# A two-block network on one core: the recurrence taken two tokens at a time, and a tail that keeps channels on partitions

## The reference

```python
w = jnp.exp(-jnp.exp(time_decay + jnp.tanh(xw @ td_w1) @ td_w2)).reshape(b, l, h, s_)
r, k, v = (xr @ Wr.T), (xk @ Wk.T), (xv @ Wv.T)          # each reshaped to (b, l, h, s_)
g = jax.nn.silu(xg @ Wg.T)
def step(s, rkvw):
    r_t, k_t, v_t, w_t = rkvw
    a = k_t[..., :, None] * v_t[..., None, :]
    out = jnp.einsum('bhi,bhij->bhj', r_t, u * a + s)
    s = a + w_t[..., :, None] * s
    return (s, out)
m = og.mean(-1, keepdims=True)                            # og: out, per head of 16 channels
va = ((og - m) ** 2).mean(-1, keepdims=True)
og = ((og - m) / jnp.sqrt(va + 1e-05)).reshape(b, l, e) * gn_w + gn_b
x1 = x + og * g @ Wo.T
xc = _ln(x1, ln2_w, ln2_b)
# shift by one token, two mixes xk2 and xr2, then:
rr = jax.nn.sigmoid(xr2 @ Wfr.T)
kk = jnp.square(jax.nn.relu(xk2 @ Wfk.T))
return x1 + rr * (kk @ Wfv.T)
```

## Time and profile before

| | us |
|---|---|
| median of 3 runs | 1902.09 (1901.77 to 1902.61) |
| the profiled execution, whole | 1903.22 |
| its span, first to last instruction | 1901.3 |

### The profile page before, as it was taken

How to read it: one execution, slowest core, us unless ns; L and a number is a source line. 1 busy time by engine, 2 the same in 40 slices (tenths; PEclk the granted TensorE clock), 3 DMA queues, 4 the chain that set the end, 5 groups by cost and what they waited for, 6 DMA issues and landing times.

```text
span 1901.3 us, 34866 instructions
## 1 busy us (share of the span) xinstructions
PE 1761.4 (93%) x12356; PEld 1228.6 (65%) x12356; DVE 1775.5 (93%) x2084; ACT 1196.1 (63%) x2849; POOL 1253.3 (66%) x822
## 2 busy tenths in 40 slices
PE   5888999999999999999999999999999999999866
PEld 3666676767666677766667776666776666676533
DVE  3599999999999999999999999999999999999981
ACT  3546666666666666666666666666666666666422
POOL 1246777676777767677777766777776677776541
PEclk8899999999999999999999999999999999999878
DMA  6233433333343333333333443333443333333320
GB/s 239 60 98 96 106 102 92 101 104 102 100 106 99 92 101 104 104 101 102 99 91 102 106 106 98 103 98 91 105 107 103 98 103 96 95 107 96 91 66 11
DMA packets 86203, 189.32 MB, mean 100 GB/s; under 512 B 18800, under 2 KB 35312, under 8 KB 85008
## 3 DMA queue, kind: packets, MB, share of 16 engines
q1 hardware_dynamic: 64528, 170.32, 33.7%
q10 hardware_dynamic: 21504, 16.78, 2.7%
HBM read 161.91 MB, written 16.78 MB: 94 GB/s over the span
## 4 chain that ended last, share of the span: by engine, by line
DVE 52%; issue 24%; POOL 11%; PE 7%; ACT 6%; DVEq 0%; DMA 0%; POOLq 0%; ACTq 0%; SPq 0%
DVE S L615 18%; DVE S L606 8%; DVE S L624 8%; POOL rstd L402 7%; ACT wrep L863 3%; DVE xf L578 3%; PE bank L1004 3%; DVE nmax L521 3%; DVE xx L568 2%; PE bank L1011 1%; DVE xin L531 1%; POOL rstd L400 1%; DVE st L663 1%; DVE x L659 1%; POOL S L446 1%
## 5 line engine op out<-in xcount | busy, mean ns | idle before, releaser
L615 DVE TENSOR_TENSOR_SCAN S<-wrep,S 128x1024 f32<-128x1024 f32 x256 | 602.6, 2354 | 2.1 <-ACT wrep L863 0.8
L446 POOL COPY S<-s 128x8 f32<-128x8 f32 x256 | 281.4, 1100 | 291.9 <-PE bank L1129 283.3
L624 DVE TENSOR_TENSOR S<-S,rT 128x1024 f32<-128x1024 f32 x256 | 343.3, 1341 | 2.8 <-ACT rT L868 1.6
L606 DVE TENSOR_TENSOR S<-vrep,kT 128x1016 f32<-128x1016 f32 x256 | 341.0, 1332 | 0.0
L430 POOL TENSOR_TENSOR xf<-xf,xa 128x512 f32<-128x512 f32 x160 | 249.3, 1558 | 89.8 <-DVE xf L578 87.5
L402 POOL TENSOR_TENSOR rstd<-rstd,mhalf 128x1 f32<-128x1 f32 (+1 forms) x96 | 211.3, 2201 | 8.0
L1129 PE MATMUL bank<-S,slide 128*32 128x256 f32 x2048 | 165.0, 394 | 23.8 <-DVE S L624 23.7
L827 ACT ACTIVATE bank<-bank,par 128x128 f32<-128x128 f32 x640 | 175.8, 366 | 10.6 <-PE bank L1085 10.6
L402 POOL TENSOR_TENSOR hrs<-hrs,mhalf 128x32 f32<-128x32 f32 x32 | 174.8, 5462 | 2.7
L400 POOL TENSOR_SCALAR rstd<-mv 128x1 f32<-128x1 f32 (+1 forms) x96 | 36.2, 377 | 204.9 <-DVE mv L542 151.8
L790 ACT ACTIVATE prob<-bank,nmax 128x512 f32<-128x512 f32 x128 | 88.3, 690 | 102.4 <-DVE nmax L521 101.5
(11 more groups left out here) (131 smaller groups left out, 3763.3 us busy)
## 6 DMA issues: line engine op xcount, KB each, us to landing
vrep<-v_dram SPq DMA_DIRECT2D x256, 512.0 KB
xc<-x_c SPq DMA_DIRECT2D x32, 256.0 KB, 6.4
xs<-x_s SPq DMA_DIRECT2D x32, 256.0 KB, 7.1
v_dram<-vT ACTq DMA_DIRECT2D x32, 256.0 KB, 2.3
xres<-xin SPq DMA_DIRECT2D x32, 256.0 KB, 6.1
out<-rr ACTq DMA_DIRECT2D x32, 256.0 KB, 2.0
Wv<-big_w SPq DMA_DIRECT2D x1, 1024.0 KB, 7.3
Wk<-big_w SPq DMA_DIRECT2D x1, 1024.0 KB, 9.3
```

The costliest lines, as they stand in the source:

```text
L446: po.tensor_copy(S[:, u % 2, :, 0], s0[:, p, k:k + UJ]).then_inc(pool_wkv.sem, 1)
L606: ve_.tensor_tensor(S[:, u % 2, :, 1:P], vrep[:, u % 2, :, 0:P - 1], k, ALU.mult).then_inc(dve_wkv.sem, 1)
L615: ve_.tensor_tensor_scan(s, wrep[:, u % C, :, :].rearrange("p j t -> p (j t)"), s, 0.0, ALU.mult, ALU.add).then_inc(dve_wkv.sem, 1)
L624: ve_.tensor_tensor(s, s, rT[:, p, u % C, :].unsqueeze(1).broadcast_to([P, UJ, P]), ALU.mult).then_inc(dve_wkv.sem, 1)
```

## The change

Three things are changed, and the orders written out by hand are redone to suit.

1. The recurrence runs over pairs of tokens. The outer products go into a tile `A` of 128 tokens, with the key of each first token already multiplied by the second token's decay (`mid_kw`); `wkv_pair` adds the two of each pair into a tile `S` of 64 columns; the scan runs over 64 pairs with the product of two decays (`ez2`, made on GpSimd, and a plain copy in `decay`); `wkv_read` reads each state twice, once with the receptance of the first token and once with that of the second times the first's decay (`mid_rw`), and writes into `A`. What the pair's first token gives the second directly (`rk2`) goes through `tail_C` with the bonus.
2. The tail keeps channels on partitions. The channels of a head are laid out in another order (`by_j`, by a permutation of `Wv`, `Wg`, `Wo` and the norm's parameters on the host), so that the bank of sums already has the wanted layout. The bonus is added to it on VectorE (`tail_o`, `tail_o2`, `tail_ob`, `tail_os`), the squares are summed over heads on TensorE (`tail_Vr`), ScalarE adds eps and spreads the factor (`tail_hv`, `tail_hp`), one transpose (`tail_Rs`) turns it, `tail_gn` multiplies. `tail_To`, `tail_Tg`, `tail_o4`, `tail_var` are gone. The free PSUM bank joins the ring of the back stages.
3. The attention's output has three buffers in place of the DMA copy; the store of `v` is four DMAs in place of one.

```diff
 FRONT_JOBS = [(j, int(lag)) for j, lag in (x.split(":") for x in (
-    "Tx:1 Mn:0 V:0 Mm:0 W1:1 S0:0 Wt:1 S1:0 S2:0 Mv:1 Mw:1 S3:0 Mk:1 Mr:1 Mg:1 Vp:1 D1:1 Kp:1 "
-    "T0:0 T1:0 T2:0 T3:0 O:0 D2:1 E2:1 Rp:1 G:1").split())]
+    "Mn:0 Wt:1 V:0 Mm:0 Mv:1 Mw:1 S0:0 S1:0 S2:0 Vp:1 Mk:1 Mr:1 Mg:1 S3:0 D1:1 Kp:1 D2:1 E2:1 "
+    "Rp:1 T0:0 T1:0 T2:0 T3:0 O:0 G:1 Tx:0 W1:0").split())]
...
-    "FR:4 FV:4 Tg:3 Wo:3 Tx2:3 FK:3 C:2").split())]
-FRONT_BANKS, BACK_BANKS, SUM_BANK, O_BANK = [0, 1, 2, 3], [6, 7], 4, 5
+    "Vr:3 FV:4 Rs:3 Wo:3 Tx2:3 FK:3 C:2 FR:3").split())]
+FRONT_BANKS, BACK_BANKS, SUM_BANK = [0, 1, 2, 3], [5, 6, 7], 4
...
+            def mid_ez2(n, m, p):
...
+                po.tensor_tensor(ez2[:, :, :], first(ez[:, :, :]), second(ez[:, :, :]), ALU.mult).then_inc(pool_ez2.sem, 1)
...
+            def wkv_rk2(n, m, p):
...
+                po.tensor_tensor(rk2[:, :, :], second(rT[:, :, :]), first(kT[:, :, :]), ALU.mult).then_inc(pool_rk2.sem, 1)
...
+            def mid_kw(n, m, p):
...
+                ve_.tensor_tensor(first(kt[:, p, :, :]), first(kT[:, :, :]), second(ez[:, :, :]),
+                                  ALU.mult).then_inc(dve_pre.sem, 1)
+
+            def mid_rw(n, m, p):
...
+                ve_.tensor_tensor(second(rt[:, p, :, :]), second(rT[:, :, :]), first(ez[:, :, :]),
+                                  ALU.mult).then_inc(dve_pre.sem, 1)
...
-                k = kT[:, p, u % C, 0:P - 1].unsqueeze(1).broadcast_to([P, UJ, P - 1])
-                ve_.tensor_tensor(S[:, u % 2, :, 1:P], vrep[:, u % 2, :, 0:P - 1], k, ALU.mult).then_inc(dve_wkv.sem, 1)
+                k = kt[:, p, u % C, 0:P - 2].unsqueeze(1).broadcast_to([P, UJ, P - 2])
+                ve_.tensor_tensor(A[:, u % 2, :, 0:P - 2], vrep[:, u % 2, :, 0:P - 2], k, ALU.mult).then_inc(dve_outer.sem, 1)
+
+            def wkv_pair(n, m, p, u):
+
+                eng.wait_ge(dve_outer.sem, dve_outer.count(f"a{u}", n))
+                a = A[:, u % 2, :, 0:P - 2]
+                ve_.tensor_tensor(S[:, u % 2, :, 1:T2], first(a), second(a), ALU.add).then_inc(dve_pair.sem, 1)
...
-                s = S[:, u % 2, :, :]
-                ve_.tensor_tensor(s, s, rT[:, p, u % C, :].unsqueeze(1).broadcast_to([P, UJ, P]),
-                                  ALU.mult).then_inc(dve_wkv.sem, 1)
+                out4 = A[:, u % 2, :, :].rearrange("p j (m k) -> p j m k", k=2)
+                s = S[:, u % 2, :, :].unsqueeze(3).broadcast_to([P, UJ, T2, 2])
+                r = rt[:, p, u % C, :].rearrange("p (m k) -> p m k", k=2).unsqueeze(1).broadcast_to([P, UJ, T2, 2])
+                ve_.tensor_tensor(out4, s, r, ALU.mult).then_inc(dve_read.sem, 1)
...
+            def tail_o2(n, m, p):
...
+                ve_.tensor_tensor(pv[:, :, :], first(vT[:, p, :, :]), over_chunks(bank_of("C")[:, P:P + T2]),
+                                  ALU.mult).then_inc(dve_tail.sem, 1)
+
+            def tail_ob(n, m, p):
...
+                ve_.tensor_tensor(b2, b2, pv[:, :, :], ALU.add).then_inc(dve_tail.sem, 1)
+
+            def tail_os(n, m, p):
...
+                ve_.tensor_tensor(oc[:, :], bank[SUM_BANK][:, :], oc[:, :], ALU.add).then_inc(dve_tail.sem, 1)
...
-                sc.activation(wrep[:, c, :, 1:P], ez[:, c, 0:P - 1].unsqueeze(1).broadcast_to([P, UJ, P - 1]),
-                              ACT.Exp, scale=-1.0).then_inc(act_decay.sem, 1)
+                sc.activation(wrep[:, c, :, 1:T2], ez2[:, c, 0:T2 - 1].unsqueeze(1).broadcast_to([P, UJ, T2 - 1]),
+                              ACT.Copy).then_inc(act_decay.sem, 1)
...
                 for c in range(C):
-                    last = pe.matmul(bank_of("C")[:, c * P:(c + 1) * P], head_u[:, c, :], rku[:, c, :],
-                                     start=True, stop=True)
+                    pe.matmul(bank_of("C")[:, 0:P], head_u[:, c, :], rku[:, c, :], start=(c == 0), stop=(c == C - 1))
+                for c in range(C):
+                    last = pe.matmul(bank_of("C")[:, P:P + T2], heads_of[:, c, :], rk2[:, c, :],
+                                     start=(c == 0), stop=(c == C - 1))
...
+            def tail_Vr(n, m, p):
...
+                for c in range(C):
+                    last = pe.matmul(bank_of("Vr")[:, 0:H], sq[:, c * P:(c + 1) * P], head_sum[:, :],
+                                     start=(c == 0), stop=(c == C - 1))
...
+            def tail_Rs(n, m, p):
...
+                pe.transpose(bank_of("Rs")[:, 0:P], hrep[:, :], ident[:, :]).then_inc(pe_tail.sem, 1)
```

The new order on TensorE, with the place of the sums among the other jobs:

```diff
+                if b0: att_M(*b0, 0)
+                if b1: mid_Wt(*b1)
+                if b0: att_V(*b0)
+                if b3: tail_Vr(*b3)
                 if b2: wkv_sum(*b2, 0)
...
+                if b1: mid_P(*b1, "r", "Rp", "Wr")
+                if b2: wkv_sum(*b2, 5)
...
+                if b1: mid_P(*b1, "g", "G", "Wg")
+                if b2: wkv_sum(*b2, 7)
+
                 if b3: tail_FK(*b3)
+                if b0: mid_Tx(*b0)
                 if b2: tail_C(*b2)
...
+                if b3: fin_FR(*b3)
+                if b0: mid_W1(*b0)
```

More of the change, by code:

```diff
@@ L31 @@
 U = C * HS // UJ
-CONSTS = 14 + C
+T2 = P // 2
+CONSTS = 16 + 3 * C
 LAGS = 5
@@ L106, in build @@
         mhalf = sb("mhalf", [P, H])
+        head_sum = sb("head_sum", [P, H])
+        eps = sb("eps", [P, 1])
         par = sb("par", [P, NPAR])
@@ L146, in build @@
         ez = sb("ez", [P, C, P])
[L147 to L150, removed]
+        kT = sb("kT", [P, C, P])
+        rT = sb("rT", [P, C, P])
+        kt = sb("kt", [P, 2, C, P])
+        rt = sb("rt", [P, 2, C, P])
+        ez2 = sb("ez2", [P, C, T2])
+        wrep = sb("wrep", [P, C, UJ, T2])
         vT = sb("vT", [P, 2, C, P])
@@ L179, in by_chunk, with first, second @@
             return ap.rearrange("p (c t) -> p c t", c=C)
+        def first(ap):
+            return ap.rearrange("p c (m k) -> p c m k", k=2)[:, :, :, 0]
+        def second(ap):
+            return ap.rearrange("p c (m k) -> p c m k", k=2)[:, :, :, 1]
         xn = prob[:, 0, :]
@@ L691, in step @@
                 if b3: tail_o(*b3)
-                if b2: wkv_read(*b2, 0)
-                if b2: wkv_outer(*b2, 1)
-                if b0: att_rstd(*b0)
-                if b3: tail_var(*b3)
-                if b2: wkv_scan(*b2, 1)
-                if b2: mid_gate(*b2)
-                if b2: wkv_read(*b2, 1)
+                if b3: tail_o2(*b3)
                 if s == 1: centre_wv()
                 if b1: mid_shift(*b1)
+                if b0: att_rstd(*b0)
+                if b3: tail_ob(*b3)
@@ L703, in step @@
+                if b1: mid_xx(*b1)
+                if b2: wkv_pair(*b2, 1)
+                if b2: wkv_read(*b2, 0)
+                if b3: tail_os(*b3)
+                if b2: wkv_scan(*b2, 1)
+                if b2: wkv_read(*b2, 1)
+                if b1: mid_s0(*b1)
                 if b2: wkv_outer(*b2, 2)
-                if b1: mid_xx(*b1)
+                if b2: wkv_outer(*b2, 3)
+                if b2: wkv_pair(*b2, 2)
+                if b2: wkv_pair(*b2, 3)
                 if b2: wkv_scan(*b2, 2)
+                if b1: mid_mix(*b1, 0)
@@ L755, in step @@
-                if b1: wkv_outer(*b1, 0)
             run(step)
@@ L936, in step @@
                 b0, b1, b2, b3, b4 = on
+                if b2: mid_k(*b2)
+                if b2: mid_ez(*b2)
+                if b1: att_scale(*b1, 3)
+                if b2: mid_w(*b2)
+                if b4: tail_xhat(*b4)
+                if b2: mid_r(*b2)
+                if b1: att_probT(*b1, 0)
+                if b1: att_probT(*b1, 1)
+                if b1: att_probT(*b1, 2)
+                if b1: att_probT(*b1, 3)
+                if b4: tail_xc2(*b4, 0)
+                if b4: tail_xc2(*b4, 1)
```

429 lines of the change are left out of this document (226 added, 203 removed).

## The result

The changed kernel takes 1919.64 us (median of 4 runs, 1916.18 to 1920.41) against 1901.93 (4 runs): ratio 1.0090, 95% interval 1.0075 to 1.0105. The forecast was 1859 with a range from 1818 to 1918, so it is slower where faster was forecast. (TensorE is PE in the rows, VectorE is DVE, ScalarE is ACT, GpSimd is POOL, and SP is the engine that issues most of the DMAs.)

A forecast was written before the change was run, and what follows sets the result against it. VectorE (55.13 of 55.66 us a step) bounds the kernel, TensorE close behind; after, TensorE at 54.4. 36 us from 29 full steps plus 7 from three lighter ones: 1903.2 - 43 = 1860, median 1859 us, range 1818 to 1918.

The forecast's parts named there:

- At nothing: ScalarE's extra work, including three more store issues at 0.4 us each, hidden by its 18 us of room a step.
- a step set by ScalarE's order, which I have not priced as a chain: Listed sign of a wrong forecast: ScalarE's instruction order sets the step; no size given.
- VectorE waiting for the biases: How ScalarE's extra work would show in VectorE if its room did not cover it; no size given.
- the main term: 29 full steps, each going from 55.65 to 54.4 us as TensorE becomes the bound: 36 us less.
- The pair sum and the small strided operations: VectorE's stride-two reads priced by output elements: pair sum 0.60 us (bounds 0.60 to 1.13), 256-element operations 0.34 each.
- The rival in which the stride is paid: VectorE's strided pair sums and small operations cost 5.3 us more a step: 58.5 us, 1994 us in all; chance 7%.
- TensorE's new matmuls: Added matmuls in tail_C and tail_Vr taken at 0.9 us each, near their weight loads; TensorE net +0.6 a step.
- the rival in which short matmuls go by columns: TensorE at 53.4 us, VectorE's gain arrives whole, step 53.2 to 53.4: 1825 us; chance 18%.
- The exclusion with GpSimd: VectorE operations lengthened beside GpSimd's: loss left at 2.56 us a step; rival where it grows, 1946 us, chance 12%.
- The start, the ramp and the drain: Three steps without all stages gain VectorE's 2.4 us each, 7 us; the drain's changed chain about even.
- The waits: VectorE idles 1 to 2 us at outer product 7 for sum 5, costing nothing while TensorE is the bound.
- The rival of two engines waiting for each other: TensorE keeps 1 to 1.8 us of idle through VectorE handshakes: step centre 55.7, 1895 us; chance 17%.

The follow-up runs named there:

- e3: The kernel before, with its one store of v cut into four of 32 partitions at the same place: 1902.24 us, ratio 0.9998.
- e1: The changed kernel, with the four stores of v issued by SP near the start of its next step instead of by ScalarE: 1872.95 us, ratio 0.9845.
- e4: The changed kernel with one matmul of tail_Vr in place of four, leaving out three quarters of each head's squares: 1904.19 us, ratio 1.0008.
- e6: The changed kernel with two of the four stores of v on ScalarE in their place and two on SP: 1881.61 us, ratio 0.9892.
- e2: The changed kernel with the four stores still on ScalarE, but behind mid_dt, after the last bias: 1878.03 us, ratio 0.9867.
- e8: e1 with tail_Vr's head sums as four 32-column-group matmuls, a ScalarE copy and one adding matmul, full computation: 1863.62 us, ratio 0.9795.
- e9: e8 with the two sums of tail_C joined, GpSimd also multiplying by u, full computation: 1848.93 us, ratio 0.9716 to the kernel before.
- e7: e1 with VectorE's tail_o2 and tail_ob cut to 4 elements, leaving out the pair's direct term: 1869.52 us, ratio 0.9831.

## Why the prediction was wrong

**The step that failed** is the part headed "At nothing": the four stores of `v` were priced at "three more issues (0.4 us each if like the one now)" and taken as hidden, because ScalarE has 18 us of room a step. Both halves were off. The four issues took 2.5 to 3.0 us in the steps looked at (median of a single one 0.62), against 0.37 for the one before. And room in the step is no cover at a place: the 3.3 us of idle that hid the store before (e3) stood behind `mid_v` in the old order; in the new one three biases stand there, with 1.7 us to spare in e1 (0.5 of idle before the bias, 1.2 until VectorE comes for it). 3.0 less 1.7 is 1.3, and the step after is 1.3 us longer than e1's (55.67 against 54.37). The prediction looked for whoever waits for the data (`vrep`, much later) and not for what is queued behind the instruction. It named "a step set by ScalarE's order, which I have not priced as a chain" as what would make it wrong, and "VectorE waiting for the biases" as what ScalarE's extra would show as without cover; both came true.

The price of this step is after against e1: 46.7 of the 60.6 us between 1859 and 1919.64. The other 14 are in e1 too. To see where, take the start of unit 1's outer product in blocks 0, 1 and 30 as marks. The text on the earlier trace rows calls its rows at 132.76 and 1745.72 unit 1; by the order of the kernel they are unit 0 (the first of the run is at 77.11), which changes nothing in the 55.62 us a step that was read from them. Before, after and e1:

```profile
83.89 1.21 DVE L606 TENSOR_TENSOR S<-vrep,kT 128x1016 f32<-128x1016 f32 x1
...
140.13 1.21 DVE L606 TENSOR_TENSOR S<-vrep,kT 128x1016 f32<-128x1016 f32 x1
...
1752.36 1.20 DVE L606 TENSOR_TENSOR S<-vrep,kT 128x1016 f32<-128x1016 f32 x1
```

```profile
92.64 1.19 DVE L654 TENSOR_TENSOR A<-vrep,kt 128x1008 f32<-128x1008 f32 x1
...
148.13 1.19 DVE L654 TENSOR_TENSOR A<-vrep,kt 128x1008 f32<-128x1008 f32 x1
...
1762.55 1.20 DVE L654 TENSOR_TENSOR A<-vrep,kt 128x1008 f32<-128x1008 f32 x1
```

```profile
90.27 1.19 DVE L662 TENSOR_TENSOR A<-vrep,kt 128x1008 f32<-128x1008 f32 x1
...
140.99 1.19 DVE L662 TENSOR_TENSOR A<-vrep,kt 128x1008 f32<-128x1008 f32 x1
...
1717.60 1.20 DVE L662 TENSOR_TENSOR A<-vrep,kt 128x1008 f32<-128x1008 f32 x1
```

| us | to block 0 | to block 1 | 29 steps | to the end |
|---|---|---|---|---|
| before | 83.9 | 56.2 | 1612.2 | 148.9 |
| after | 92.6 | 55.5 | 1614.4 | 156.1 |
| e1 | 90.3 | 50.7 | 1576.6 | 153.7 |

Unit 1 stands elsewhere in the new order, so a few us may belong in a neighbouring column; the sum of the three columns beside the 29 steps is free of that.

**The full steps.** With the stores off ScalarE the 29 steps are 35.6 us shorter than before; the forecast said 36. So the main term was right, mechanism and size, and was hidden: in the changed kernel as it is, the same steps are 2.2 us longer than before. (All five stages are there in 28 steps; the prediction's 29 counts one that is nearly full.)

**The pair sum and the small strided operations** went by elements of the output, 0.57 and 0.34, the lower bound taken. The rival in which the stride is paid falls. The rule of the Trainium skill ("Advanced Engine Details and Errata", Memory Cachelines) that two hits on a 16-byte line give full speed agrees with this trace: at 8 bytes from element to element the pair sum of 504 elements took 0.57, where contiguous rows of 512 take 0.60.

**TensorE's new matmuls**: 0.84 and 0.91 for eight instructions of 64 and 32 columns, where 0.9 each was taken (bounds 0.25 to 0.97). They cost about what their weight loads do, as assumed, so the rival in which short matmuls go by columns falls. The step of e1, 54.44, is TensorE's busy time and nothing else, as the forecast's 54.4.

**The exclusion with GpSimd** did not grow. Three operations a step are lengthened in the changed kernel as before:

```profile
902.50 2.02 DVE L654 TENSOR_TENSOR A<-vrep,kt 128x1008 f32<-128x1008 f32 x1
...
907.51 2.19 DVE L654 TENSOR_TENSOR A<-vrep,kt 128x1008 f32<-128x1008 f32 x1
...
934.84 1.72 DVE L669 TENSOR_TENSOR_SCAN S<-wrep,S 128x512 f32<-128x512 f32 x1
```

0.8, 1.0 and 0.5 us over their like, 2.3 against 2.56. The first two stand in the circle shown with e4, between the mix of the key and sum 5. In e1 the step's losses are about 1 us smaller (VectorE busy 51.61 against 52.82), which e6 shows is not what most of its gain rests on.

**The start, the ramp and the drain** were put at 7 us of gain and "about even". In e1 the start is 6.4 us longer than before, the step from block 0 to block 1 is 5.5 shorter, and the end is 4.8 longer: 5.6 us more where 7 less were forecast, 13 us worse. That is nearly all of the difference of e1 (1873) from 1859. Part of it is seen: before the first outer product VectorE in e1 waits 6.0 us for the decays (`mid_w`), which `mid_kw` needs, where before only the scan needed them. How the rest divides stays open.

**The waits** forecast for VectorE at outer product 7 for sum 5 (1 to 2 us) are in e1, 1.30 us a step, and cost nothing there. The rival of two engines waiting for each other gave a step of 55.7, and the step after is 55.67, but that the numbers meet is luck: the wait came through a third engine, not by the handshakes that it named, and with the stores off ScalarE TensorE has no idle at all in the step.

## What to carry over

A DMA's issue is an instruction of the engine that issues it: it belongs in the sum with its own duration, which is not that of a DMA of another shape. It is hidden only by what stands right behind it in that engine's order: idle time there, and the time by which the next results would be early. When an order is rearranged, look for the wait that used to stand behind each such instruction, and if it has gone, move the issue to a place that has one (e2) or to an engine that can take it (here SP: VectorE's waits for `vrep` came to 0.7 us in all of e1, 0.9 after). When two engines are both near full, a gain on one is worth only what the other lets through: after VectorE's 2.4 us the next two gains (e8, e9) came from TensorE, where matmuls of few columns with full weights were cheap to remove, while taking 0.5 us from VectorE left the full steps as they were (e7).

## What the runs showed of the hardware

- A store of 32 partitions x 4 x 512 bytes took ScalarE 0.48 us to issue when each partition's four rows lay 64 KB apart and neighbouring partitions' rows side by side (1.92 for four), 0.63 to 0.74 us with rows of neighbouring partitions 16 rows apart (2.52 to 2.97 for four; median of a single one 0.62), once 0.9 (1.89 for two, e6). One store of 128 partitions, with four times the bytes, took 0.37. So the time of an issue does not go by bytes. What stood behind the stores in ScalarE's order waited for them: its next operation began 0.04 us after the last issue's end. An operation ahead of an issue can still run beside it: in e2 the tanh of `mid_dt` ran from 935.75 for 0.28 us, and the issues began at 935.80.
- Stride on VectorE was free at 8 bytes (0.57 us for 504 elements) and not at 128: the reduction that centres `Wv` took 2.28 us for 2048 contiguous elements before, 3.56 in the changed kernel, where its elements are 32 apart, and 3.55 in e1:

```profile
37.80 3.55 DVE L592 TENSOR_REDUCE sx<-Wv 128x128 f32<-128x2048 f32 x1
```

- Eight TensorE instructions with 128 x 128 fp32 weights cost 0.91 us at 32 columns, 0.84 at 64, 0.89 at 128 (927.57 to 928.46; 0.99 before) and 1.30 at 192. With 128 x 32 weights, in four groups of 32 columns of the array side by side, eight cost 0.24 at 128 columns (e8).
